# Segment sum of a GNN edge stage: one edge tile in eight as two fp32r products instead of one fp32 product

## The chip, the cores and the metric

One core of a Trainium2 chip runs the whole program in one launch. The metric is the device time in microseconds, median of the runs.

## The reference, cut to what matters

The model is a GNN message-passing layer, a mixture-of-experts feed-forward, two SAGE convolutions and a routed feed-forward over 3125 nodes of 256 features and 53125 edges. The change lies in the first of them, in the messages and their sum by node:

```python
msg_input = jnp.concatenate([node_i, node_j, edge_features], axis=-1)
h = jax.nn.relu(msg_input @ mW1 + mb1)
messages = h @ mW2 + mb2
aggregated = jax.ops.segment_sum(messages, i_idx, num_segments=n)
```

The kernel sums h by target node first and multiplies by mW2 afterwards, so its segment sum is over rows of 512 hidden values, together with the number of edges of each node.

## The kernel before, in words

Earlier stages sort the edges by target node into buckets of 96 nodes (SB = 96) and leave, in memory, p (the target node's part of the hidden layer, one table of 128x512 a bucket: 96 nodes and twice 16 rows of edge weights), q (the source node's part, one row of 512 a node), and records of 34 words a slot: target place, source number, and the edge's features twice, rounded to fp32r and as the rests. The function stage_sort_and_edges then runs over 240 groups (NGS) of 256 slots, which are two tiles of 128 each; tile t = 2g + j belongs to group g. For each group:

- SyncE loads the records (rb, line 848, one load for four groups, three buffers) and stores the group's running sum (agg, line 863).
- GpSimd gathers the q rows of a tile by an indirect DMA (qg, line 887). There are six buffers, so the gather of tile t waits for the add of tile t - 6 (line 884).
- VectorE builds the one-hot matrix of the target places (one_hot, line 949, two SBUF inputs), adds the hidden product and the gathered rows (line 973), and carries the running sum on (accumulate, line 959: old sum times keep, plus p_sum).
- ScalarE copies the edge features beside the one-hot (widen, line 906), takes the transposed matrix from PSUM as fp32r (take, line 910), applies relu in place on hb (line 933) and carries the degree column (line 920).
- TensorE transposes wide (line 983), forms the hidden product with the fp32r high and low part of p (line 993, two products a tile) and the segment sum (line 1004: one-hot, 128x96, as the stationary side, hb, 128x512, as the moving side, one fp32 product a tile; two tiles accumulate into one of two p_sum banks).

The order of the work on each engine is written out by hand. TensorE's loop over groups is: transposes(g+1), hidden(g), sums(g-1). VectorE's is: accumulate(g-2), one_hot(g+2), add of tile 2g, add of tile 2g+1. ScalarE's is: widen(g+2), take(g+1), relu of 2g and 2g+1, degrees(g). Each engine runs its own in order and waits on semaphores; p_h has four banks, p_sum two, wide six buffers, hb four, agg four. The next stage (line 1203 and on) begins when the last store of agg is in.

Of the kernel before, what the change touches and what calls it, by code (L numbers as in the profile page):

```python
# [6 lines left out]
ALU = mybir.AluOpType  # L7
ACT = mybir.ActivationFunctionType
AX = mybir.AxisListType
F32 = mybir.dt.float32  # L10
F32R = mybir.dt.float32r
# [6 lines left out]
P = 128  # L18
# [3 lines left out]
HID = 512  # L22
# [14 lines left out]
SB = P - 2 * EDGE_DIM  # L37
NBS = -(-N_NODES // SB)
NGS = (N_EDGES + NBS * (GROUP - 1)) // GROUP
# [757 lines left out]
def stage_sort_and_edges(nc, C, A, S):  # L797
# [3 lines left out]
    with ExitStack() as ctx:  # L801
        m = Mem(nc, ctx)
# [3 lines left out]
        RB, QB, XB, HB, AB = 3, 6, 6, 4, 4  # L806
        PC = 11
        PB = NBS // PC
        LOAD = 4
        p_low, p_high = m.sb("p_low", [P, NBS, HID], F32R), m.sb("p_high", [P, NBS, HID], F32R)  # L810
        rb = [m.sb(f"rb{b}", [P, BT, REC]) for b in range(RB)]
        wide = [m.sb(f"wide{b}", [P, 2, P]) for b in range(XB)]
        trs = [m.sb(f"trs{b}", [P, 2, P], F32R) for b in range(2)]
        qg = [m.sb(f"qg{b}", [P, HID]) for b in range(QB)]
        hb = [m.sb(f"hb{b}", [P, HID]) for b in range(HB)]
        agg = [m.sb(f"agg{b}", [SB, HID + 1]) for b in range(AB)]
        deg_g = m.sb("deg_g", [P, AB])
        p_tr = [m.ps(f"p_tr{b}", [P, 2, P]) for b in range(2)]
        p_h = [m.ps(f"p_h{b}", [P, HID]) for b in range(4)]
        p_sum = [m.ps(f"p_sum{b}", [P, HID]) for b in range(2)]  # L820
# [5 lines left out]
        s_wide, s_hot, s_tr, s_trs = m.sem("e_wide"), m.sem("e_hot"), m.sem("e_tr"), m.sem("e_trs")  # L826
        s_h, s_add, s_relu, s_sum = m.sem("e_h"), m.sem("e_add"), m.sem("e_relu"), m.sem("e_sum")
        s_first, s_acc, s_deg = m.sem("e_first"), m.sem("e_acc"), m.sem("e_deg")
        recs_v = S.recs[0:NSLOTS, :].rearrange("(n p r) w -> n p r w", p=P, r=BT)
        p_v = S.p[0:NBS * P, :].rearrange("(b p) n -> p b n", p=P)  # L830
        agg_v = S.agg.rearrange("(b p) w -> b p w", p=SB)

        def records_in(eng, g):

            n = g // (BT // 2)
            eng.wait_ge(s_rec[n % RB], 16 * (n // RB) + 16)
            return rb[n % RB], 2 * g % BT

        def flushed(eng, g):

# [3 lines left out]
        with nc.Block() as block:  # L844
            @block.sync
            def _(sp):
# [11 lines left out]
                for g in range(NGS):  # L858
                    if g % LOAD == 0:
                        dest = load_own_buckets(nc, sp, C.dest[0:1, g:g + LOAD], NBS + NGS)  # L860
                    sp.wait_ge(s_acc, g + 1)
                    sp.wait_ge(s_deg, g + 1)
                    sp.dma_start(agg_v[bass.ds(dest[g % LOAD], 1)].rearrange("a p w -> (a p) w"),
                                 agg[g % AB][:, :]).then_inc(s_flush[g % AB], 16)
# [27 lines left out]
            @block.scalar  # L892
            def _(act):
                sort.scalar(act)
                act.wait_ge(C.s_table_read, 1)
                act.activation(C.ident_r[:, :], C.ident[:, :], ACT.Copy).then_inc(s_high, 1)
                for c in range(PC):
                    some = slice(c * PB, (c + 1) * PB)
                    act.wait_ge(s_p[c], 16)
                    act.activation(p_high[:, some, :], p_low[:, some, :].bitcast(F32), ACT.Copy).then_inc(s_high, 1)  # L900

                def widen(g):
                    src, at = records_in(act, g)
                    if g >= XB:
                        act.wait_ge(s_sum, g - XB + 1)
                    act.activation(wide[g % XB][:, :, SB:P], src[:, at:at + 2, 2:REC], ACT.Copy).then_inc(s_wide, 1)  # L906

                def take(g):
                    act.wait_ge(s_tr, g + 1)
                    act.activation(trs[g % 2][:, :, :], p_tr[g % 2][:, :, :], ACT.Copy,  # L910
                                   accum_out=deg_g[:, g % AB:g % AB + 1]).then_inc(s_trs, 1)

                def degrees(g):
                    act.wait_ge(s_trs, g + 1)
                    if g == 0:
                        act.wait_ge(s_first, 1)
                    else:
                        act.wait_ge(s_deg, g)
                    flushed(act, g)
                    act.activation(agg[g % AB][:, HID:HID + 1], agg[(g - 1) % AB][:, HID:HID + 1], ACT.Identity,  # L920
                                   bias=deg_g[0:SB, g % AB:g % AB + 1], scale=C.keep[0:SB, g:g + 1]).then_inc(s_deg, 1)

                widen(0)
                widen(1)
                take(0)
                for g in range(NGS):
                    if g + 2 < NGS:
                        widen(g + 2)
                    if g + 1 < NGS:
                        take(g + 1)  # L930
                    for t in (2 * g, 2 * g + 1):
                        act.wait_ge(s_add, t + 1)
                        act.activation(hb[t % HB][:, :], hb[t % HB][:, :], ACT.Relu).then_inc(s_relu, 1)  # L933
                    degrees(g)

            @block.vector
            def _(dve):
                sort.vector(dve)
                for b in range(NBS):
                    dve.wait_ge(s_copy, b + 1)  # L940
                    dve.tensor_tensor(p_low[:, b, :], p_low[:, b, :].bitcast(F32), p_h[b % 4][:, :],
                                      ALU.subtract).then_inc(s_low, 1)
                iota = C.iota_f[:, 0:SB].rearrange("p (a n) -> p a n", a=1)

                def one_hot(g):
                    src, at = records_in(dve, g)
                    if g >= XB:
                        dve.wait_ge(s_sum, g - XB + 1)
                    dve.tensor_tensor(wide[g % XB][:, :, 0:SB], iota.to_broadcast([P, 2, SB]),
                                      src[:, at:at + 2, 0:1].to_broadcast([P, 2, SB]), ALU.is_equal).then_inc(s_hot, 1)  # L950

                def accumulate(g):
                    dve.wait_ge(s_sum, g + 1)
                    if g == 0:
                        dve.wait_ge(s_first, 1)
                    else:
                        dve.wait_ge(s_acc, g)
                    flushed(dve, g)
                    dve.scalar_tensor_tensor(out=agg[g % AB][:, 0:HID], in0=agg[(g - 1) % AB][:, 0:HID],  # L959
                                             scalar=C.keep[0:SB, g:g + 1], in1=p_sum[g % 2][0:SB, :],  # L960
                                             op0=ALU.mult, op1=ALU.add).then_inc(s_acc, 1)

                one_hot(0)
                one_hot(1)
                for g in range(NGS):
                    if g >= 2:
                        accumulate(g - 2)
                    if g + 2 < NGS:
                        one_hot(g + 2)
                    for t in (2 * g, 2 * g + 1):  # L970
                        dve.wait_ge(s_h, t + 1)
                        dve.wait_ge(s_gath[t % QB], 16 * (t // QB) + 16)
                        dve.tensor_tensor(hb[t % HB][:, :], p_h[t % 4][:, :], qg[t % QB][:, :], ALU.add).then_inc(s_add, 1)  # L973
                accumulate(NGS - 2)
                accumulate(NGS - 1)

            @block.tensor
            def _(pe):
                def transposes(g):
                    pe.wait_ge(s_wide, g + 1)  # L980
                    pe.wait_ge(s_hot, g + 1)
                    for j in range(2):
                        last = pe.transpose(p_tr[g % 2][:, j, :], wide[g % XB][:, j, :], C.ident[:, :])  # L983
                    last.then_inc(s_tr, 1)

                def hidden(g, bucket):
# [11 lines left out]
                def sums(g):  # L998
                    if g >= 2:
                        pe.wait_ge(s_acc, g - 1)  # L1000
                    for j in range(2):
                        t = 2 * g + j
                        pe.wait_ge(s_relu, t + 1)
                        last = pe.matmul(p_sum[g % 2][0:SB, :], wide[g % XB][:, j, 0:SB], hb[t % HB][:, :],  # L1004
                                         start=(j == 0), stop=(j == 1))
                    last.then_inc(s_sum, 1)

                sort.tensor(pe)
# [8 lines left out]
                for g in range(NGS):  # L1017
                    if g % LOAD == 0:
                        buckets = load_own_buckets(nc, pe, C.bucket[0:1, 0, g:g + LOAD], NBS - 1)
                    if g + 1 < NGS:  # L1020
                        transposes(g + 1)
                    hidden(g, buckets[g % LOAD])
                    if g > 0:
# [1148 lines left out]
```

## Time and profile before

| what | value |
| --- | --- |
| median of 3 runs | 2958.7 us (2958.1 to 2959.84) |
| the profiled execution | 2963.02 us |
| its span | 2960.8 us |
| busy in the span: PE, DVE, ACT, POOL | 2468.8, 1909.6, 1019.1, 1809.9 us |
| segment-sum products, line 1004 | 960 records (two to an fp32 product), first at 607.6, last at 1296.7 us |
| bytes moved, mean rate | 446.46 MB, 151 GB/s |

How to read it: the edge stage covers some 690 of the 2961 us, from 607 to 1297. PE is TensorE's products and PEld its weight loads, DVE is VectorE, ACT ScalarE, POOL GpSimd, SP SyncE; a letter q behind an engine is its queue of DMA issues. Times are us from the start of the span. PEclk is the granted clock of TensorE as a share of full speed. Matmuls are pipelined: their starts are what counts, while the durations given overlap the next one.

### The profile page before, as it was taken

The numbers are of one execution on the slowest core, as the hardware profiler recorded it, in microseconds if no ns is written. First come the engines' busy times: TensorE is split into PE (matmuls) and PEld (weight loads), VectorE is DVE, ScalarE is ACT, GpSimd is POOL, SyncE is SP. The second block draws the span as 40 slices with busy tenths as digits, with TensorE's granted clock in tenths as the row PEclk, the third lists the DMA queues.
The fourth block names the chain that finished last, engine by engine and source line by source line (L and its number), as shares of the span: only waits on it lengthen the run. The fifth ranks groups of instructions, "written<-read, shape, count | busy, mean of one in ns | idle before, by whom it ended". The sixth has DMA issues, their size and how long they took to land. (4 is left out here: it accounts for less than half of the span.)

```text
span 2960.8 us, 35471 instructions
## 1 busy us (share of the span) xinstructions
PE 2468.8 (83%) x8644; PEld 1444.2 (49%) x8644; DVE 1909.6 (64%) x3873; ACT 1019.1 (34%) x2851; POOL 1809.9 (61%) x1880
## 2 busy tenths in 40 slices
PE   5588997289999999989998858888777777778799
PEld 2144443045555555546666645555444444343577
DVE  8997876267777777744535656666654444444888
ACT  1277778157776777742222210000110000000232
POOL 5777777767676767630037757777547777777200
PEclk8799999589999999999999989999777777876899
DMA  9222324079999999982056665555343333333001
GB/s 281 72 84 85 96 88 160 14 218 269 263 264 266 262 263 265 266 245 74 27 167 204 201 191 168 169 169 166 94 133 106 105 105 106 106 105 105 22 1 45
DMA packets 238394, 446.46 MB, mean 151 GB/s; under 512 B 47451, under 2 KB 129005, under 8 KB 237999
## 3 DMA queue, kind: packets, MB, share of 16 engines
q0 software_dynamic: 96288, 254.83, 31.9%
q1 hardware_dynamic: 136416, 184.09, 19.0%
q10 hardware_dynamic: 5488, 5.28, 0.5%
q8 instruction: 75, 1.23, 0.2%
q14 instruction: 127, 1.03, 0.1%
HBM read 320.06 MB, written 126.13 MB: 151 GB/s over the span
## 5 line engine op out<-in xcount | busy, mean ns | idle before, releaser
L1780 POOL DMA_INDIRECT nbr_yg<-y_d,gidx x763 | 721.6, 946 | 245.4 <-PE nbr_sum L1890 130.7
L1890 PE MATMUL nbr_sum<-nbr_yg,nbr_hot 128*128 128x258 f32 x1526 | 603.9, 503 | 216.3 <-DMA nbr_yg<-y_d,gidx 169.9
L887 POOL DMA_INDIRECT qg<-q_d,rb x480 | 481.8, 1004 | 207.7 <-DVE hb L973 114.3
L1828 DVE TENSOR_TENSOR nbr<-nbr_sum,nbr 128x258 f32 x763 | 323.6, 424 | 435.6 <-PE nbr_sum L1890 411.4
L1890 PEld LDWEIGHTS nbr_sum<-nbr_yg,nbr_hot 128*128 128x128 f32 x1526 | 299.8, 232 | 503.6 <-DMA nbr_yg<-y_d,gidx 187.9
L413 POOL DMA_INDIRECT recs_d<-recs,slot_src x416 | 409.5, 984 | 150.3 <-issue 138.5
L1004 PE MATMUL p_sum<-hb,wide 128*96 128x512 f32 x960 | 452.1, 593 | 2.6 <-ACT hb L933 2.6
L933 ACT ACTIVATE hb<-hb 128x512 f32<-128x512 f32 x480 | 295.9, 630 | 208.8 <-DVE hb L973 207.3
L973 DVE TENSOR_TENSOR hb<-p_h,qg 128x512 f32<-128x512 f32 x480 | 310.1, 680 | 21.6 <-DMA qg<-q_d,rb 20.0
L1278 POOL DMA_INDIRECT n_ahead<-y_d,gidx x165 | 156.7, 949 | 268.2 <-DMA y_d<-n_y 200.6
L437 ACT ACTIVATE lane_hot<-bare_hot,val 128x128 f16<-128x128 f16 x832 | 247.5, 392 | 123.5 <-DVE bare_hot L671 123.5
L959 DVE SCALAR_TENSOR_TENSOR agg<-agg,keep,p_sum 96x512 f32<-96x512 f32 x240 | 178.3, 743 | 141.2 <-PE p_sum L1004 140.8
L664 DVE TENSOR_TENSOR col_hot<-p_iota,col 128x3712 f16<-128x3712 f32 x52 | 209.0, 4019 | 45.4 <-PE acc L726 45.4
L1004 PEld LDWEIGHTS p_sum<-hb,wide 128*96 128x96 f32 x960 | 155.8, 163 | 158.6 <-issue 125.7
L726 PE MATMUL acc<-col_hot,lane_hot 128*128 128x464 f16 x832 | 173.1, 361 | 65.9 <-ACT lane_hot L437 65.8
L993 PE MATMUL p_h<-p_high,trs 128*128 x480 | 211.1, 440 | 0.0
L1955 ACT ACT_TABLE_LOAD x1 | 1.3, 1283 | 591.0 <-PEq L1749 591.0
L993 PE MATMUL p_h<-p_low,trs 128*128 x480 | 190.9, 398 | 0.0
L983 PEld LDWEIGHTS p_tr<-ident,wide 128*128 128x128 f32 x480 | 67.7, 142 | 201.4 <-issue 132.0
L726 PEld LDWEIGHTS acc<-col_hot,lane_hot 128*128 128x128 f16 x832 | 79.8, 98 | 152.1 <-issue 42.6
L983 PE MATMUL p_tr<-ident,wide 128*128 128x128 f32 x480 | 92.7, 275 | 68.0 <-ACT wide L906 68.0
L1799 DVE TENSOR_TENSOR nbr_hot<-nbr_iota,dloc 128x1024 f32<-128x1024 f32 (+2 forms) x171 | 144.4, 872 | 0.1
(321 smaller groups left out, 3466.5 us busy)
## 6 DMA issues: line engine op xcount, KB each, us to landing
agg_d<-agg SPq DMA_DIRECT2D x240, 192.4 KB, 5.2
msg_d<-n_ahead SPq DMA_DIRECT2D x165, 128.0 KB, 2.7
nbr_ys<-msg_d SPq DMA_DIRECT2D x165, 128.0 KB, 2.5
nbr_yg<-y_d,gidx POOLq DMA_INDIRECT x763, 2.8
p_low<-p_d SPq DMA_DIRECT2D x11, 768.0 KB, 12.4
recs_d<-fill SPq DMA_DIRECT2D x16, 510.0 KB
rb<-recs_d SPq DMA_DIRECT2D x60, 136.0 KB, 4.9
qg<-q_d,rb POOLq DMA_INDIRECT x480
```

Of the source, the lines that this page charges most:

```text
L413: pool.indirect_dma_start(S.recs[:, :], bass.IndirectOffsetOnAxis(ap=slot_src[:, c:c + 1], axis=0), recs[:, c, :], None).then_inc(s_scat, 16)
L437: last = act.activation(lane_hot[g % TBUF][:, j, k, :], bare_hot[g % BARE][:, j, :], ACT.Copy, scale=val[:, k, TC * g + j:TC * g + j + 1])
L664: dve.tensor_tensor(col_hot[b][:, :, :], cols_iota.to_broadcast([P, TC, NCOL]), col[:, TC * g:TC * g + TC, :].to_broadcast([P, TC, NCOL]), ...
L726: last = pe.matmul(acc[k][:, 0:NCOL], lane_hot[b][:, j, k, :], col_hot[b][:, j, :], start=False, stop=False)
L887: pool.indirect_dma_start(qg[t % QB][:, :], None, S.q[:, :], bass.IndirectOffsetOnAxis(ap=rb[n % RB][:, t % BT, 1:2].bitcast(U32), axis=0) ...
L933: act.activation(hb[t % HB][:, :], hb[t % HB][:, :], ACT.Relu).then_inc(s_relu, 1)
L973: dve.tensor_tensor(hb[t % HB][:, :], p_h[t % 4][:, :], qg[t % QB][:, :], ALU.add).then_inc(s_add, 1)
L993: last = pe.matmul(p_h[t % 4][:, :], trs[g % 2][:, j, :], part[:, bass.ds(bucket, 1), :].rearrange("p a n -> p (a n)"), start=(part is p_h ...
L1004: last = pe.matmul(p_sum[g % 2][0:SB, :], wide[g % XB][:, j, 0:SB], hb[t % HB][:, :], start=(j == 0), stop=(j == 1))
L1780: pool.indirect_dma_start(yg[n % YB][:, 0:D], None, S.y[:, :], bass.IndirectOffsetOnAxis(ap=C.gidx[:, FROM + n:FROM + n + 1], axis=0)).the ...
L1828: dve.tensor_tensor(nbr, p_sum[t % SUMS][:, 0:W], nbr, ALU.add).then_inc(s_acc, 1)
L1890: pe.matmul(p_sum[t % SUMS][:, 0:W], hot[t // BT % HOTS][:, column, :], rows[:, :], start=True, stop=True).then_inc(s_sum, 1)
```

## The change

The relu of every eighth tile (t % 8 == 1) is written to a new tile h_high in fp32r, which rounds it. VectorE then forms h_low as max(hb, 0) minus h_high, also in fp32r, at the next group, between one_hot and the adds. TensorE multiplies the one-hot by h_high and by h_low, in fp32r, into the same sum. The wide tiles are declared fp32r for that, and read as fp32 elsewhere. h_high and h_low have two buffers each, with waits on the sums of the split two before. The other seven tiles in eight are as they were.

```diff
-        LOAD = 4
+        LOAD, EACH_SPLIT = 4, 4
-        wide = [m.sb(f"wide{b}", [P, 2, P]) for b in range(XB)]
+        wide = [m.sb(f"wide{b}", [P, 2, P], F32R) for b in range(XB)]
+        h_high = [m.sb(f"h_high{b}", [P, HID], F32R) for b in range(2)]
+        h_low = [m.sb(f"h_low{b}", [P, HID], F32R) for b in range(2)]
...
+        def is_split(t):
+            return t % (2 * EACH_SPLIT) == 1
...
-                        act.activation(hb[t % HB][:, :], hb[t % HB][:, :], ACT.Relu).then_inc(s_relu, 1)
+                        into = hb[t % HB]
+                        if is_split(t):
+                            n = g // EACH_SPLIT
+                            if n >= 2:
+                                act.wait_ge(s_sum, EACH_SPLIT * (n - 2) + 1)
+                            into = h_high[n % 2]
+                        act.activation(into[:, :], hb[t % HB][:, :], ACT.Relu).then_inc(s_relu, 1)
...
+                def low_part(t):
+                    dve.wait_ge(s_relu, t + 1)
+                    n = t // (2 * EACH_SPLIT)
+                    if n >= 2:
+                        dve.wait_ge(s_sum, EACH_SPLIT * (n - 2) + 1)
+                    dve.scalar_tensor_tensor(out=h_low[t // (2 * EACH_SPLIT) % 2][:, :], in0=hb[t % HB][:, :], scalar=0.0,
+                                             in1=h_high[t // (2 * EACH_SPLIT) % 2][:, :].bitcast(F32), op0=ALU.max,
+                                             op1=ALU.subtract).then_inc(s_h_low, 1)
...
                     if g + 2 < NGS:
                         one_hot(g + 2)
+                    if g > 0 and is_split(2 * g - 1):
+                        low_part(2 * g - 1)
...
-                        last = pe.transpose(p_tr[g % 2][:, j, :], wide[g % XB][:, j, :], C.ident[:, :])
+                        last = pe.transpose(p_tr[g % 2][:, j, :], wide[g % XB][:, j, :].bitcast(F32), C.ident[:, :])
...
-                        last = pe.matmul(p_sum[g % 2][0:SB, :], wide[g % XB][:, j, 0:SB], hb[t % HB][:, :],
-                                         start=(j == 0), stop=(j == 1))
+                        if is_split(t):
+                            hot = wide[g % XB][:, j, 0:SB]
+                            pe.matmul(p_sum[g % 2][0:SB, :], hot, h_high[t // (2 * EACH_SPLIT) % 2][:, :], start=(j == 0), stop=False)
+                            pe.wait_ge(s_h_low, t // (2 * EACH_SPLIT) + 1)
+                            last = pe.matmul(p_sum[g % 2][0:SB, :], hot, h_low[t // (2 * EACH_SPLIT) % 2][:, :], start=False, stop=(j == 1))
+                        else:
+                            last = pe.matmul(p_sum[g % 2][0:SB, :], wide[g % XB][:, j, 0:SB].bitcast(F32), hb[t % HB][:, :],
+                                             start=(j == 0), stop=(j == 1))
```

## Rows read from the trace of the kernel before

**Rows 1.** By stretch: window, length, engines' busy us (count), PEclk, DMA share, GB/s.

```profile
640.00:740.00 100.00, 100.00 (x351) 55.12 (x350) 77.41 (x140) 70.38 (x210) 70.07 (x71) 1.00 0.90 264
...
940.00:1040.00 100.00, 100.00 (x350) 54.91 (x349) 78.37 (x141) 71.72 (x214) 70.03 (x70) 1.00 0.96 265
1040.00:1140.00 100.00, 99.04 (x345) 54.20 (x344) 77.03 (x140) 69.27 (x208) 69.25 (x70) 1.00 0.96 263
```

**Rows 2.** Waits, 640 to 1240 us: total us, times, longest us.

```profile
ACT hb L933 <- DVE hb L973: 177.8, 224, 2.8
DVE agg L959 <- PE p_sum L1004: 120.3, 193, 0.7
...
POOL qg L887 <- DVE hb L973: 102.5, 186, 2.8
...
DVE hb L973 <- DMA qg<-q_d,rb: 14.1, 24, 2.8
...
PE p_sum L1004 <- ACT hb L933: 1.0, 1, 1.0
```

**Rows 3.** Timeline of one group, 900 to 906 us: start, us, engine, line.

```profile
900.01 1.88 PE L1004 MATMUL p_sum<-hb,wide 128*96 128x512 f32 x4
...
901.72 0.38 PE L983 MATMUL p_tr<-ident,wide 128*128 128x128 f32 x2
...
901.92 0.74 DVE L959 SCALAR_TENSOR_TENSOR agg<-agg,keep,p_sum 96x512 f32<-96x512 f32 x1 [0.66 <-PE p_sum L1004]
...
902.59 0.35 DVE L949 TENSOR_TENSOR wide<-iota_f,rb 128x192 f32<-128x192 f32 x1
...
902.67 1.08 POOL L887 DMA_INDIRECT qg<-q_d,rb  x1 [0.30 <-issue]
902.86 1.28 DVE L973 TENSOR_TENSOR hb<-p_h,qg 128x512 f32<-128x512 f32 x2
902.87 1.88 PE L1004 MATMUL p_sum<-hb,wide 128*96 128x512 f32 x4
...
903.57 1.23 ACT L933 ACTIVATE hb<-hb 128x512 f32<-128x512 f32 x2 [0.85 <-DVE hb L973]
...
904.28 0.94 POOL L887 DMA_INDIRECT qg<-q_d,rb  x1 [0.53 <-DVE hb L973]
...
904.59 0.38 PE L983 MATMUL p_tr<-ident,wide 128*128 128x128 f32 x2
...
905.74 1.88 PE L1004 MATMUL p_sum<-hb,wide 128*96 128x512 f32 x4
```

**Rows 4.** Timeline, PE alone, the stage's last groups, where no transposes are left.

```profile
1291.08 1.88 PE L1004 MATMUL p_sum<-hb,wide 128*96 128x512 f32 x4
...
1293.03 0.40 PE L993 MATMUL p_h<-p_low,trs 128*128 x1
1293.26 0.39 PE L993 MATMUL p_h<-p_high,trs 128*128 x1
...
1293.49 0.39 PE L993 MATMUL p_h<-p_low,trs 128*128 x1
...
1293.72 3.60 PE L1004 MATMUL p_sum<-hb,wide 128*96 128x512 f32 x8
```

**Rows 5.** Lines 1986, 2021, 2030 by tile: ns min/median/max, first and last start.

```profile
L1986 DVE SCALAR_TENSOR_TENSOR last_junk<-last_XN,last_wr x25: 412/416/2940, 2765.7 to 2828.0; 128x256 f32<-128x256 f32 x25
...
L2021 DVE SCALAR_TENSOR_TENSOR z<-last_b,last_gate,z x25: 479/480/485, 2930.9 to 2940.4; 128x256 f32<-128x256 f32 x25
...
L2030 DVE SCALAR_TENSOR_TENSOR x<-last_out,last_gate,z x5: 479/484/484, 2948.7 to 2956.6; 128x256 f32<-128x256 f32 x5
```

**Rows 6.** Timeline of POOL and DVE around two gathers.

```profile
1091.83 0.95 POOL L887 DMA_INDIRECT qg<-q_d,rb  x1 [0.46 <-DVE hb L973]
...
1092.99 0.35 DVE L949 TENSOR_TENSOR wide<-iota_f,rb 128x192 f32<-128x192 f32 x1
...
1093.08 1.08 POOL L887 DMA_INDIRECT qg<-q_d,rb  x1 [0.30 <-issue]
```

**Rows 7.** By stretch of 20 us, columns as in rows 1.

```profile
960.00:980.00 20.00, 20.00 (x71) 11.02 (x70) 15.50 (x29) 14.05 (x43) 14.24 (x14) 1.00 0.97 254
...
1240.00:1260.00 20.00, 20.00 (x72) 10.97 (x71) 15.82 (x29) 14.20 (x42) 14.53 (x15) 1.00 0.99 282
```

**Rows 8.** The operation that writes fp32r on DVE, by tile p_low.

```profile
L941 DVE TENSOR_TENSOR p_low<-p_low,p_h x33: 681/682/687, 515.4 to 534.5; 128x512 fp32r<-128x512 f32 x33
```

More of the change, by code:

```diff
@@ L828, in stage_sort_and_edges @@
         s_first, s_acc, s_deg = m.sem("e_first"), m.sem("e_acc"), m.sem("e_deg")
+        s_h_low = m.sem("e_h_low")
         recs_v = S.recs[0:NSLOTS, :].rearrange("(n p r) w -> n p r w", p=P, r=BT)
@@ L973, in _ @@
                         dve.tensor_tensor(hb[t % HB][:, :], p_h[t % 4][:, :], qg[t % QB][:, :], ALU.add).then_inc(s_add, 1)
+                assert not is_split(2 * NGS - 1)
                 accumulate(NGS - 2)
```

## The prediction

> **What bounds the kernel now.** The table by stretch comes first [rows 1]. In the edge stage PE is busy for all of each 100 us (99.04 in one stretch) at a granted clock of 1.00, the 2.4 GHz level, while DVE stands at 77 to 78%, ACT at 69 to 72% and POOL at 69 to 70%. The second thing to see there is the DMA column: 0.90 to 0.96 for 263 to 265 GB/s. The waits of the same stage [rows 2] agree: DVE waits for the sums of PE 193 times, ACT and POOL wait for DVE, and PE itself waited once for ACT, 1.0 us in 600. DVE waited for a gather 24 times among 418 tiles, 14.1 us in all. So PE sets the pace, DVE follows it, and the transfers are the next limit.
>
> One group in order of time [rows 3] gives the pace. PE starts its transposes at 901.72 and the next ones at 904.59, a period of 2.87 us, or 2.865 as a mean over the two periods between the sums of 900.01 and 905.74. The sums of the group before start at 902.87 and end where the next transposes begin, 904.59: 1.72 us for four records, two to a product, so 0.43 us a record and 0.86 us an fp32 product. DVE does the accumulation (901.92), the one-hot (902.59) and two adds (902.86), is through at 904.14, and then idles 0.66 us until the next sums are there.
>
> **The change, part by part.** Tiles 1, 9, 17 and so on to 473 are split, 60 of 480, always the second of their group.
>
> *PE.* A split tile loses one fp32 product and gets two fp32r products on the same 512 columns. Fp32r products of this width stand in the trace as the hidden products. Near the end of the stage they follow fp32 sums with no transpose between [rows 4]: four fp32 records start at 1291.08, four fp32r products follow, and the next sums start at 1293.72. That is 2.64 us, and 4 x 0.43 leaves 0.92 us for the four, 0.23 us each; the neighbours at 1293.03, 1293.26 and 1293.49 are also 0.23 apart. So going from one kind to the other costs nothing that can be seen. The split tile takes 2 x 0.23 = 0.46 us in place of 0.86 and saves 0.40 us. Times 60: 24.0 us. The stationary side has 96 columns where the hidden products have 128; no row has fp32r with 96, and nothing makes fewer columns dearer.
>
> *The low part on DVE.* It is a scalar_tensor_tensor over 128x512 with a constant as scalar and two inputs in SBUF. Its rows are of 256 elements [rows 5]: 480 ns with a scalar per partition (line 2021), 416 ns with a constant (line 1986). The accumulation, 512 elements, takes 0.74 us [rows 3], so 256 more elements cost 0.26 us, and the low part comes to 0.416 + 0.263 = 0.68 us, in the row of DVE some 0.61 us because neighbours overlap (two adds of 0.68 take 1.28). What two SBUF inputs do to the rate can be read too: line 2021 has both inputs in SBUF and 480 ns, line 2030 takes one from PSUM and has 484 ns [rows 5]. So I take 0.68.
> The Trainium skill, "Vector Engine (DVE) Microarchitecture Reference", section "Points that are easy to get wrong", says the opposite for this form: two SBUF sources that aren't bf16 halve its throughput. The rows don't bear it out, and what it would give is the third rival.
>
> *Where that lies.* Take the accumulation's start, 901.92, as 0. DVE in a group after a split tile: accumulation 0, one-hot 0.67, low part 0.94 to 1.62, adds at 1.55 and 2.15, through at 2.83 in place of 2.22. The low part waits for the second relu of the previous pair, whose pair started at 900.70 (the row at 903.57 less one period) and ended at 901.93, time 0.01: 0.9 us early. PE: the sums start at 0.95, the first tile ends at 1.81, the high product at 2.04, and the low product needs the low part of 1.62. Spare: 0.4 us, less a semaphore's way (0.07 from an add's end to relu). Behind that waiting product stand the next transposes and hidden products; by this count they don't wait. The transposes start at 2.27 instead of 2.67. The next accumulation could start at 2.47, but DVE is free at 2.76, so it takes the place of the 0.66 us idle. Nobody on PE misses it: there are two sum buffers. Adds of the next group then start at 3.70, their relus end by 5.6, and the sums that take them start at 5.15 plus 1.15 us of transposes and hidden products, 6.3. DVE is back in step after one group: in four groups it works 4 x 2.2 + 0.61 = 9.4 us of 4 x 2.865 - 0.40 = 11.06.
>
> *The small edits.* The relu of a split tile writes another tile; ACT waits for DVE 30% of the stage (177.8 of 600 us) [rows 2], which would hide another 0.1 us a split; without that cover it would be 6 us in all. The one-hot and the widening write fp32r instead of fp32: an fp32r output of DVE takes 682 ns [rows 8] where the fp32 one took 0.68, so nothing. The extra waits on sums two splits back were met eight groups, some 20 us, before. No DMA is added, moved or taken away.
>
> *Gathers and DMA.* Adds 0.61 us later in one group of four free their buffers later. A gather starts at 904.28 [rows 3] after the add that ended at 903.50, and its tile is added three periods after 902.86, at 911.46: 7.2 us, of which the change takes 0.2 (shorter periods) and at most 0.6 after a split. POOL can issue every 1.25 us [rows 6], 10.0 us for the eight gathers of 11.06. Bytes per group stay, so the rate rises by 11.46/11.06, 3.6%, to 273 GB/s. Bounds for what the transfers then give: one stretch moved 282 GB/s at a share of 0.99, another 254 at 0.97 [rows 7], which scaled to a full share is 285 (all of the gain fits) and 262 (none does). The mean of the dense stretch 940 to 1140 is 264 at 0.96, 275 at full share, against 273 wanted: 99% full. If those 200 us gained nothing, it would cost 200 x 3.5% = 7.0 us; if all of the stage, 24.0. I take a third of 7.0, 2.3 us, because that stretch is the nearest row and its own figure still just fits.
>
> **Sum.** 24.0 - 2.3 = 21.7 us, all in the edge stage; the next stage begins when this one's last stores are in and moves ahead as a block. The profiled execution took 2963.0 us (span 2960.8), and would take 2941.3. It lies 4.3 us over the median of 2958.7, so for the median I forecast 2937.0.
>
> **The rivals.**
> 1. *The transfers take half of it.* DMA full over most of the stage: the gain stays between 6 and 18 us, 2941 to 2953, with 12 as its middle, 2947. For it: the share of 0.96 and 24 waits. Against: shares of 0.90 with the same bytes early in the stage.
> 2. *Slower, through the gathers.* A gather that starts under DVE's one-hot, which reads two SBUF tiles, takes 1.08 us; the one before it takes 0.95 [rows 6]. The low part reads two SBUF tiles for 0.68 us and follows straight on the one-hot, so the gather at 902.67 could be held some 0.6 us more. POOL's next one starts 0.53 us after it is free, which hides nearly all. But where gathers are what DVE waits for, each split costs 0.6 us in place of the 0.40 gained; that makes the kernel slower if it is so at more than 40% of the splits (0.40 / 1.00). Now it is at 24 of 418, 6%. At 60%: 60 x (0.36 - 0.16) = 12 us slower, 2971; at all of them 36 us, 2995.
> The Trainium skill, "SBUF — State Buffer", section "SBUF: two separate sides", calls the pair of ports between VectorE and GpSimd an exclusive lock, also for a VectorE operation with two SBUF inputs against a GpSimd one that reads SBUF; by that rule the gather waits out the low part, and the 1.08 us row agrees in kind.
> 3. *The low part takes twice the time per element*: 0.15 + 512 x 2 x 1.03 ns = 1.2 us. It is then ready at 2.14, PE waits about 0.2 us at 2.04, and half is left: 12 us, 2947. Lines 2021 and 2030 speak against it.
> 4. *The two products aren't cheap*: at 0.43 us each nothing is gained, 2959. The hidden products in the same type and width at 0.23 speak against it.
>
> **How the numbers follow.** Forecast 2937 (2933 to 2940): 0.62. Rival 1: 0.22. Rival 2: 0.08. Rival 3: 0.03. Rival 4 or a gain eaten whole: 0.05. A measurement of this kernel tells about 0.2%, 6 us, from no change. Faster is the forecast with rivals 1 and 3, less 0.02 for their thin ends: 0.85; same 0.07; slower 0.08. The range starts at 2932, the whole 24.0 us with 3 us for a different mean, and goes to 2950, which takes in the larger part of rivals 1 and 3.
>
> **What would show it.** Records of the split sums 0.23 us apart, 60 fp32 products fewer; groups of 2.87, 2.87, 2.87 and 2.47 us in turn; PE still busy throughout, 36.1 groups per 100 us for 34.9; a low part of 0.68 us; DVE's 0.66 us idle gone once in four groups; GB/s at 273. It is wrong if PE waits for the low part, if DVE's waits for gathers grow from 14 us to more than 30, or if GB/s stays at 265.

## The result, and the profile after

The changed kernel takes 2950.99 us (median of 8 runs, 2948.84 to 2954.76) where the kernel before takes 2960.02 us in the same comparison. The ratio is 0.9965, with a 95% interval of [0.9954, 0.9976]: faster by 9 to 10 us, less than half of the 22 that were forecast, and 1 us outside the range.

In the two profiled executions the span went from 2960.8 to 2948.0 us. All of it is in the edge stage. By the tile of the group sums, first and last accumulation, for the kernel before:

```profile
L959 DVE SCALAR_TENSOR_TENSOR agg<-agg,keep,p_sum x240: 732/743/746, 611.5 to 1297.4; 96x512 f32<-96x512 f32 x120
```

and after:

```profile
L971 DVE SCALAR_TENSOR_TENSOR agg<-agg,keep,p_sum x240: 727/742/746, 611.5 to 1284.2; 96x512 f32<-96x512 f32 x120
```

Both stages start at the same time, and the last accumulation comes 13.2 us earlier. The stage took 685.9 us and takes 672.7.

Was the work on PE priced right? A group after a split tile, in an undisturbed part of the stage (timeline after; line 1007 is the transposes, 1030 and 1032 the high and the low product, 980 the low part, 996 the adds):

```profile
720.69 0.38 PE L1007 MATMUL p_tr<-ident,wide 128*128 128x128 f32 x2
...
720.89 0.74 DVE L971 SCALAR_TENSOR_TENSOR agg<-agg,keep,p_sum 96x512 f32<-96x512 f32 x1 [0.65 <-PE p_sum L1034]
...
721.82 0.69 DVE L980 SCALAR_TENSOR_TENSOR h_low<-hb,h_high 128x512 fp32r<-128x512 f32 x1
721.83 1.02 PE L1034 MATMUL p_sum<-hb,wide 128*96 128x512 f32 x2
...
722.29 0.80 PE L1030 MATMUL p_sum<-h_high,wide 128*96 128x512 f32 x1
722.44 1.27 DVE L996 TENSOR_TENSOR hb<-p_h,qg 128x512 f32<-128x512 f32 x2
...
722.92 0.39 PE L1032 MATMUL p_sum<-h_low,wide 128*96 128x512 f32 x1
...
723.15 0.38 PE L1007 MATMUL p_tr<-ident,wide 128*128 128x128 f32 x2
...
723.64 0.73 DVE L971 SCALAR_TENSOR_TENSOR agg<-agg,keep,p_sum 96x512 f32<-96x512 f32 x1
```

From transposes to transposes it takes 2.46 us, where rows 3 have 2.87. The sums take 723.15 - 721.83 = 1.32 us, which is 2 x 0.43 + 2 x 0.23. (The record of the high product starts before the fp32 product ahead of it is through, so high and low stand 0.63 us apart in the rows and not 0.23; it is the sum of 1.32 us that tells the price.) The low part starts 0.93 us after the accumulation, and PE does not wait for it: the whole group runs as the prediction had it. Successive high products stand 11.05 us apart there.

Where the gain went, then, is in the waits. The stage of after, 640 to 1240 us, beside rows 2:

```profile
ACT hb L945 <- DVE hb L996: 139.4, 185, 1.8
...
DVE hb L996 <- DMA qg<-q_d,rb: 49.5, 66, 2.1
DVE agg L971 <- PE p_sum L1034: 44.1, 86, 0.7
...
PE p_sum L1034 <- ACT hb L945: 4.3, 6, 1.0
PE p_sum L1032 <- DVE h_low L980: 2.7, 9, 0.4
```

DVE's waits for gathers went from 14.1 us in 24 to 49.5 us in 66. Its waits for PE fell from 120.3 to 44.1: it has lost the slack that used to take such a wait in. And by stretch, beside rows 1:

```profile
640.00:740.00 100.00, 99.12 (x355) 55.50 (x354) 84.05 (x151) 71.59 (x212) 70.92 (x71) 1.00 0.91 269
...
940.00:1040.00 100.00, 99.39 (x359) 56.10 (x358) 84.95 (x153) 72.59 (x216) 69.14 (x72) 1.00 0.96 271
1040.00:1140.00 100.00, 97.15 (x347) 53.88 (x346) 81.42 (x147) 70.67 (x209) 69.92 (x70) 1.00 0.95 262
```

PE is no longer busy throughout (97 to 99% of each stretch) at an unchanged granted clock, and the rate is 262 to 271 GB/s, not 273. How such a stall looks (timeline after):

```profile
900.45 0.69 DVE L996 TENSOR_TENSOR hb<-p_h,qg 128x512 f32<-128x512 f32 x1 [1.01 <-DMA qg<-q_d,rb]
...
901.17 0.63 ACT L945 ACTIVATE h_high<-hb 128x512 fp32r<-128x512 f32 x1 [1.07 <-DVE hb L996]
...
901.86 0.76 PE L1030 MATMUL p_sum<-h_high,wide 128*96 128x512 f32 x1
901.89 1.59 POOL L893 DMA_INDIRECT qg<-q_d,rb  x1 [0.76 <-DVE hb L996]
...
901.98 0.68 DVE L980 SCALAR_TENSOR_TENSOR h_low<-hb,h_high 128x512 fp32r<-128x512 f32 x1
...
902.72 0.48 PE L1032 MATMUL p_sum<-h_low,wide 128*96 128x512 f32 x1
```

The gather of the split tile itself lands 1.01 us late. Its relu, the low part and the low product all come late by that, and PE starts the low product 0.86 us after the high one, where the undisturbed group has 0.63. The same rows show GpSimd: its gather issue, started 0.09 us before the low part, takes 1.59 us where one of rows 6 took 0.95.

### The profile page after: what moved, and what is told of

It reads as the page before. It is cut to its first block and busy times, and to the rows that moved or that the text cites. A ratio compares the mean times of both kernels' runs of the same rounds, so it can differ in the third digit from the quotient of the medians.

```text
span 2948.0 us, 35647 instructions
## 1 busy us (share of the span) xinstructions
PE 2434.6 (83%) x8644; PEld 1436.1 (49%) x8644; DVE 1944.1 (66%) x3933; ACT 1020.1 (35%) x2851; POOL 1805.4 (61%) x1880
## 5 line engine op out<-in xcount | busy, mean ns | idle before, releaser
L1920 PE MATMUL nbr_sum<-nbr_yg,nbr_hot 128*128 128x258 f32 x1526 | 594.4, 496 | 228.2 <-DMA nbr_yg<-y_d,gidx 182.7
L893 POOL DMA_INDIRECT qg<-q_d,rb x480 | 475.2, 990 | 201.5 <-issue 110.5
L1034 PE MATMUL p_sum<-hb,wide 128*96 128x512 f32 x840 | 401.3, 593 | 5.2 <-ACT hb L945 5.1
L996 DVE TENSOR_TENSOR hb<-p_h,qg 128x512 f32<-128x512 f32 x480 | 314.7, 681 | 60.5 <-DMA qg<-q_d,rb 58.3
L945 ACT ACTIVATE hb<-hb 128x512 f32<-128x512 f32 x420 | 261.1, 631 | 168.3 <-DVE hb L996 158.7
L1034 PEld LDWEIGHTS p_sum<-hb,wide 128*96 128x96 f32 x840 | 135.1, 162 | 132.8 <-issue 82.0
```

Source lines behind the costliest of these rows:

```text
L893: pool.indirect_dma_start(qg[t % QB][:, :], None, S.q[:, :], bass.IndirectOffsetOnAxis(ap=rb[n % RB][:, t % BT, 1:2].bitcast(U32), axis=0) ...
L945: act.activation(into[:, :], hb[t % HB][:, :], ACT.Relu).then_inc(s_relu, 1)
L1920: pe.matmul(p_sum[t % SUMS][:, 0:W], hot[t // BT % HOTS][:, column, :], rows[:, :], start=True, stop=True).then_inc(s_sum, 1)
```

## The experiments

After the result there were two theories of the lost 11 us. A: the transfers are full. B: the low part on VectorE delays the adds and, with them or through the shared port, the gathers. The first batch gave a third. C: six gather buffers are too few for the time that a gather takes, once the period is shorter. The ratios below are to the kernel before, run beside them; chips differ, so between batches only ratios are compared.

**First batch: the parts alone, and more buffers.** In e1 the low part's call is taken out of VectorE's loop, and the zeros are written once:

```diff
+                for n in range(2):
+                    dve.tensor_scalar(h_low[n][:, :], C.ones[:, 0:1].to_broadcast([P, HID]), 0.0, None, ALU.mult).then_inc(s_h_low, 1)
-                    if g > 0 and is_split(2 * g - 1):
-                        low_part(2 * g - 1)
-                            pe.wait_ge(s_h_low, t // (2 * EACH_SPLIT) + 1)
+                            pe.wait_ge(s_h_low, 2)
```

> Part alone: the changed kernel without the subtraction on VectorE. h_low is written once, with zeros, and the 60 low products read that, so the exact rest is left out of the sum. TensorE does the same work as in the changed kernel. Theory A (the transfers can't give more than they do: the shorter period alone brings the waits for gathers): time as the changed kernel, 2951, and DVE's wait for gathers stays near 58 us. Theory B (the low part on VectorE delays the adds behind it, and with them the buffers and the gathers): the whole 24 us come, 2936, and the wait for gathers falls to 30 us or less.

Measured: 0.9948 [0.9935, 0.9962], waits for gathers 83.5 us. Neither theory's number: most of the loss stays without any low part, so B can't be the main cause. It is a little better than the changed kernel, by less than the intervals tell apart. The waits themselves grew, from 58.3 us in the changed kernel, although the time did not.

e2 puts the low part into the kernel before:

```diff
+                    if g > 1 and g % 4 == 2:
+                        dve.wait_ge(s_h_low, g // 4 + 1)
+                    if g > 0 and g % 4 == 1:
+                        dve.wait_ge(s_relu, 2 * g)
+                        dve.scalar_tensor_tensor(out=h_low[g // 4 % 2][:, :], in0=hb[(2 * g - 1) % HB][:, :], scalar=0.0,
+                                                 in1=hb[(2 * g - 1) % HB][:, :], op0=ALU.max, op1=ALU.subtract).then_inc(s_h_low, 1)
```

> The other part alone: the kernel before with an operation like the low part (same form, size and place, result not used) on VectorE in one group of four; TensorE unchanged, so the period is 2.87 us. Theory A: as the kernel before, 2959 to 2960, with its 20 us of waits for gathers. Theory B: waits for gathers rise to 40 us or more in place of 20; time 0 to 6 us over the kernel before, since TensorE has 1.5 us to spare for each.

Measured: 1.0005 [0.9995, 1.0014], with 51.0 us of waits for gathers on VectorE. The waits rose as B has it; the time did not, beyond noise. At the old period nearly all of these waits end before TensorE needs the tile: from 640 to 1240 us PE waited for a relu 4 times, 2.4 us in all. A wait on VectorE is a poor measure of loss by itself.

e3 and e4 change one number, in the changed kernel and in the kernel before:

```diff
-        RB, QB, XB, HB, AB = 3, 6, 6, 4, 4
+        RB, QB, XB, HB, AB = 3, 8, 6, 4, 4
```

> The changed kernel with eight gather buffers in place of six, so that a gather can be issued 2.8 us earlier. If the loss lies in how late gathers are issued (B, or any cause by latency), it comes down to the whole gain, 2936, and the waits for gathers to under 20 us. If the transfers are full (A), the time stays at 2951, since the bytes are the same.

> The kernel before with eight gather buffers. TensorE sets its pace and lost about 1 us to gathers after the first, so both theories expect no change, 2957 to 2960; the waits for gathers on VectorE fall from 20 to under 10 us.

Measured: e3 0.9908 [0.9893, 0.9923], e4 0.9983 [0.9974, 0.9992]. The waits for gathers fall to 5.0 and 7.4 us. The group sums in both, e3 and then e4:

```profile
L971 DVE SCALAR_TENSOR_TENSOR agg<-agg,keep,p_sum x240: 728/743/746, 611.5 to 1271.1; 96x512 f32<-96x512 f32 x120
```

```profile
L959 DVE SCALAR_TENSOR_TENSOR agg<-agg,keep,p_sum x240: 733/743/746, 610.1 to 1293.8; 96x512 f32<-96x512 f32 x120
```

The stage takes 659.6 us in e3 and 683.7 in e4: in these two executions the change is worth 24.1 us where nothing else holds it, against 24.0 in the prediction's sum for PE. The medians of the runs, 2940.38 and 2962.31, are 21.9 us apart. Theory A falls too, by the stretches of e3:

```profile
640.00:740.00 100.00, 100.00 (x362) 56.85 (x361) 84.92 (x155) 72.51 (x217) 72.66 (x74) 1.00 0.94 279
940.00:1040.00 100.00, 99.41 (x360) 56.41 (x359) 84.67 (x153) 71.81 (x216) 70.45 (x72) 1.00 0.99 271
1040.00:1140.00 100.00, 100.00 (x365) 56.98 (x364) 84.58 (x154) 73.41 (x218) 71.49 (x73) 1.00 1.01 276
```

The same DMA engines move 271 to 279 GB/s once the gathers are issued earlier. e4 was not expected: the kernel before gains 5 us as well. Late gathers seem to cost it something already, though only 1.0 us of waits on PE was seen in its trace.

**Second batch: how long a gather takes.** e6 and e7 store 64 of the 513 columns of each group's sum; e5 is the changed kernel itself.

```diff
-                    sp.dma_start(agg_v[bass.ds(dest[g % LOAD], 1)].rearrange("a p w -> (a p) w"),
-                                 agg[g % AB][:, :]).then_inc(s_flush[g % AB], 16)
+                    sp.dma_start(agg_v[bass.ds(dest[g % LOAD], 1)].rearrange("a p w -> (a p) w")[:, 0:64],
+                                 agg[g % AB][:, 0:64]).then_inc(s_flush[g % AB], 16)
```

> The changed kernel itself, beside the next three on one chip, as the measure for them. 2950 to 2951 on the chip of the first comparison, 0.9965 of the kernel before; every theory expects that.

> The changed kernel with only the first 64 of 513 columns of each group's sum stored (the stores of the other columns are left out), which takes some 60 of the 270 GB/s off the DMA engines while every gather and every buffer stays. Theory C (six gather buffers are too few for the time that a gather takes under this load, once the period is shorter): gathers land sooner (5.4 us median falls under 4.5), the waits for gathers fall under 20 us, and the whole gain is there: 24 us or more under the kernel before. If the late gathers come from how POOL issues them (its port held by the low part), nothing changes: 40 us or more of waits and 10 us of gain.

> The kernel before with the same stores cut, the measure for e6. TensorE set its pace, so all theories expect 0 to 5 us less than the kernel before, in the edge stage, from the few waits for gathers that are left.

Measured: e5 0.9970 [0.9958, 0.9982], e6 0.9898 [0.9882, 0.9913], e7 0.9991 [0.9981, 1.0000]. With six buffers, and with POOL's long issues still there (14 over 1.2 us), the whole gain is back: e6 is 26.5 us under e7 in median, and its stage is 23.7 us shorter. The times from issue to landing of a gather, in the changed kernel of the first comparison and in e6:

```profile
DMA to landing us min/median/max: 3.7/5.4/7.5
```

```profile
DMA to landing us min/median/max: 3.6/4.1/5.6
```

These views pair a gather with its landing for one buffer in six, 80 of the 480 gathers. With the landing records of all six buffers the median is 5.6 us and the longest 8.35 in the changed kernel, 4.0 and 5.9 in e6, and 5.7 and 7.7 in the kernel before. So it is not that gathers got much slower; the time that they have got shorter.

How long may a gather take? The prediction's schedule gives 7.2 us with six buffers, which is right for the first gather of a group. The second one is issued 1.25 us after the first, but its tile is added only 0.6 us after the first tile. In the kernel before (line 887 the gather, 973 the add of its tile three groups later):

```profile
905.53 1.09 POOL L887 DMA_INDIRECT qg<-q_d,rb  x1 [0.30 <-issue]
...
912.06 0.68 DVE L973 TENSOR_TENSOR hb<-p_h,qg 128x512 f32<-128x512 f32 x1
```

That is 6.5 us at the old period, 6.3 by the same schedule less the prediction's 0.2, and 5.7 after a split. Gathers of up to 8.35 us don't fit in that; those of e6 just do, since its longest second gather takes 5.7 us. The waits bear it out: 20 of the 24 of before and 53 of the 66 of after, 640 to 1240 us, stand ahead of the second add of a group. The split tiles are all second tiles.

> The changed kernel with eight gather buffers and without the subtraction on VectorE (h_low holds zeros, the rest is left out). Theory C: with enough buffers the low part costs nothing, so this comes within 3 us of the changed kernel with eight buffers, 0.9908 of the kernel before. If the low part costs TensorE something by itself (a wait for h_low at each split), this is 5 us or more faster than that.

e8 is e1 with eight buffers. Measured: 0.9916 [0.9903, 0.9930], against 0.9908 for e3. With enough buffers the low part's 0.68 us costs nothing that can be measured.

**Third batch: where every version is slow.** The next four met conditions in which the kernel before took 3370.13 us.

> The changed kernel, six gather buffers, with the low part's second input read from PSUM (the hidden product of the next tile) in place of h_high in SBUF, so that h_low isn't the rest: the sums of the split tiles are other numbers. Form, length and place of the operation stay. If what the low part adds to the loss is the gather held behind it on the port shared with GpSimd, gathers of over 1.2 us vanish (26 to 29 in the changed kernel) and the time goes to that without the low part's work, 0.995 of the kernel before. If it is the 0.6 us by which the adds come later, the long gathers vanish too but the time stays at 0.997.

> Eight gather buffers and one tile in four split (120 tiles). By the count of the prediction two groups take 5.33 us; DVE works 5.0 of them and the rate wanted is 283 GB/s. If the transfers have that: another 23 us, 2917, 0.983. If they are full at the 275 to 280 GB/s seen so far: 0.986 to 0.991, with waits for gathers of 50 us or more on VectorE.

> The changed kernel with ten gather buffers. Theory C: the eight of e3 left 5 us of waits for gathers, so two more give nothing that can be measured, 0.991 of the kernel before.

> As e10 with ten gather buffers. If e10 is held by late gathers of the same kind, this gains 3 us or more on it; if the transfers are full, or VectorE is, it is the same as e10 within 3 us.

Measured: 1.0099, 1.0041, 1.0098 and 1.0057. In e11 the rate from 600 to 1300 us is 211 GB/s, the granted clock is 0.95 there where the changed kernel had 0.99, PE is busy for 596 of these 700 us, and there are waits for no cause that the profile shows. In such conditions all four were slower than the kernel before, by 0.4 to 1.0%, and the intervals leave 1 out. Why, these runs don't tell. e11 and e12 were not repeated, so whether ten buffers do more than eight is open.

**Fourth batch: how the low part adds to the loss.** e13 is e9 again, e14 is e1, e15 the changed kernel, e16 is e10 again. The edit of e13:

```diff
+                    dve.wait_ge(s_h, t + 2)
-                                             in1=h_high[t // (2 * EACH_SPLIT) % 2][:, :].bitcast(F32), op0=ALU.max,
+                                             in1=p_h[(t + 1) % 4][:, :], op0=ALU.max,
```

> As e9, on a chip and at a time where the kernel before takes 2960 to 2967 and not 3370. Six gather buffers, the low part's second input from PSUM, so h_low isn't the rest. If the low part's share of the loss is the gather held at the shared port: long gathers vanish and the ratio is that of e14, about 0.995. If it is the adds coming 0.6 us later: long gathers vanish and the ratio stays at that of e15, about 0.997.

> As e1 (h_low holds zeros, the rest is left out), for a comparison with e13 and e15 on one chip. 0.995 again: the shorter period alone, with six buffers, loses 10 us or so of the 24, and the low part's work the remaining 5.

> The changed kernel as the measure: 0.9965 to 0.9970 of the kernel before.

Measured: e13 0.9962 [0.9948, 0.9976], e14 0.9946 [0.9932, 0.9960], e15 0.9963 [0.9949, 0.9976]. GpSimd's gather issues, ns min/median/max, in e13 and in e15:

```profile
L893 POOL DMA_INDIRECT qg<-q_d,rb x480: 940/946/1127, 601.7 to 1278.4; - x160
```

```profile
L893 POOL DMA_INDIRECT qg<-q_d,rb x480: 940/946/1602, 602.2 to 1283.0; - x160
```

The long issues are gone with the second SBUF input, and the time is that of the changed kernel all the same. So the hold was real and cost nothing that can be measured. What the low part adds to the loss is some 3 to 5 us (e14 against e15 by medians and by ratios; e1 against the first result gives 5 too). That the adds come 0.6 us later would explain it; no run tests this by itself. The intervals overlap: the size of that part is an estimate.

> As e10, on a chip at its usual pace: one tile in four split, eight gather buffers. If the transfers can give 283 GB/s: 0.983. If they are full at the 275 to 280 seen so far: 0.986 to 0.991, with waits for gathers of 50 us or more.

The edit of e16 is eight gather buffers, as in e3, and

```diff
-        LOAD, EACH_SPLIT = 4, 4
+        LOAD, EACH_SPLIT = 4, 2
```

Measured: 0.9912 [0.9899, 0.9926], no better than e3. The waits for gathers are 12.9 us, not 50, so by this the transfers are not what stops it; the rate is 274 GB/s from 640 to 1240. In its trace half of the groups should take 2.46 us. Of the 216 groups from 640 to 1240 us only 66 do, counted up to 2.52; 21 lie between 2.52 and 2.83, and 55 take 2.9 to 3.05 instead of 2.87. PE stood idle before transposes 23 times for a reason that the profile calls issue, 7.4 us in all. Why, stays open.

## Why the prediction was wrong, point by point

- **What bounds the kernel**: right. PE set the pace, and what is taken off it counts in full where nothing else intervenes (e3, e6).
- **PE's saving**: right. 0.43 and 0.23 us a record held, the group of 2.46 us is there, and the 24.0 us are met: 24.1 and 23.7 us in the stages of e4 and e3, and of e7 and e6, 21.9 and 26.5 by their medians. Changing between fp32 and fp32r cost nothing, nor did 96 columns.
- **The low part**: 681 ns in the median for the predicted 680, between 678 and 729. With one of its inputs in PSUM (e13) it took 676. Rival 3, with twice the time an element, and the sentence of the Trainium skill ("Vector Engine (DVE) Microarchitecture Reference", section "Points that are easy to get wrong") that would give it, do not hold for this operation here.
- **Its place**: right in the undisturbed group. In a disturbed one it is a new tie. The add, relu, low part and low product of a split tile follow each other with little spare, where an ordinary tile had over a microsecond.
- **Gathers and DMA**: this is the step that failed. The prediction worked out the 7.2 us that a gather has from its issue to its add, took 0.2 and 0.6 off, and then never set the rest against how long a gather takes. Nor did it see that every second gather has only 6.5. It priced the step by the rate of the DMA engines instead: 2.3 us as a third of 7.0. What the runs show in its place is gathers that land too late for six buffers, and a loss of 24.1 - 13.2 = 10.9 us in the profiled executions; with eight buffers, or with gathers that land in 4 us, the loss is gone. The price of 0 to 24.0 as bounds was sound; the choice within it was not, since a full share was the wrong measure. The same engines gave 275 GB/s at a share of 0.98 in e3.
- **The 24 waits of before** were the warning. 20 of them stand ahead of a group's second add, so they said that some gathers already took longer than their 6.5 us; e7 shows the same kernel, with smaller stores, with 2 waits in the whole run, 5.4 us, when gathers land in 4.0. They were read as a sign of the rate, and are a sign of latency. Of the prediction's own signs of being wrong, waits for gathers of more than 30 us came in full; PE waited for the low part 9 times, 2.7 us in all.
- **Rival 1** forecast a gain of 6 to 18 us, and 10 came, but by another mechanism. **Rival 2** had the one that can be seen in the trace and costs nothing: 26 gather issues held for 0.3 to 0.8 us. The rule of the Trainium skill beside it ("SBUF — State Buffer", section "SBUF: two separate sides") agrees with the trace as far as a gather waits for a VectorE operation with two SBUF inputs: with one of them in PSUM (e13) the held gathers are gone. It does not agree as far as the one that starts first keeps the pair for the whole instruction: a gather issue that began 0.69 us before the low part of 991.8 and ran 0.25 us into it left that low part at 0.68 us.
- **The range** ended at 2950 to take in "the larger part" of rival 1. With the chance given to it, 0.22, it should have gone to the end of that rival, 2953. That would have taken in the measured time by luck: the mechanism of rival 1, full transfers, is refuted by e3.

## What to carry to other kernels

When work is taken off the engine that sets the pace, each ring of buffers gets less time in the same proportion. For every transfer in the stage, compare buffers times the new period, less the engines' part, with the largest time from issue to landing, not with the mean rate. A few short waits on an engine with slack are harmless by themselves, but they say which ring is at its end. And take the gather with the least time, not the first one of a group. Here two buffers more took the gain from 0.35% to 0.92%; 0.17% of that the two buffers give the kernel before by themselves. Eight gather buffers with one tile in eight split is the best of the complete versions measured, with one tile in four (e16) level with it.

## What was not expected of the hardware

- A gather's time to land depends on the load around it: 5.4 to 5.9 us in the median at 266 to 269 GB/s, 6.0 at 265 GB/s (e4) and 5.8 at 275 GB/s (e3) with eight buffers in flight, and 4.0 to 4.1 at 205 to 212 GB/s (e7, e6), with the gathers themselves unchanged. These medians are of the gathers that the view pairs.
- The share of busy time of the DMA engines is no measure of what is left. 254 GB/s stood at 0.97 and 276 GB/s at 1.01.
- A GpSimd gather issue that starts close to the start of a VectorE operation with two SBUF inputs (from 0.21 us before it to 0.26 us after) can be held by it: in the changed kernel 26 of them took 1.24 to 1.71 us in place of 0.95, and each ended 0.82 to 0.83 us after the low part did. Not each one is held: 25 others, begun between 0.18 us before the low part and 0.01 after, took 0.94 to 1.13 us, as the one beside the low part of 721.82. Then it is the VectorE operation that is a little longer: 0.69 to 0.73 us in these 25, and 0.68 beside the 26.
